# Attention and a small feed-forward block on eight cores: the last two token tiles one by one, bias rows by an accumulating DMA, query weights loaded sooner, and 53 instead of 43 tiles of exponentials on VectorE

## The reference

```python
def attn(x):                                   # x: (4, 4096, 1024)
    q = einsum('bnd,hkd->bnhk', x, query_proj) # 16 heads of 64
    k = einsum('bmd,dk->bmk', x, key_proj)     # one key head, shared
    v = einsum('bmd,dv->bmv', x, value_proj)   # one value head, shared
    p = softmax(einsum('bnhk,bmk->bnhm', q, k) / 8)
    return einsum('bnhv,dhv->bnd', einsum('bnhm,bmv->bnhv', p, v), output_proj)
def ffn(x):
    s = einsum('btd,dm->btm', x, Win) + bin_   # 64 wide
    h = relu(s[..., None] * W1 + b1)           # 16 hidden values for each
    return einsum('btm,md->btd', einsum('btmh,mh->btm', h, W2) + b2, Wout) + bout
x = x + attn(layernorm(x))
x = x + ffn(layernorm(x))
```

## Time and profile before

| | before |
|---|---|
| median of runs, us | 969.49 |
| profiled execution, us | 971.45 |
| its span, first to last instruction, slowest core | 969.9 |
| spans of the eight cores | 965.8 to 969.9 |
| ScalarE busy | 94% |
| TensorE busy | 93% |
| VectorE busy | 67% |
| GpSimd busy | 7% |
| DMA, mean | 50 GB/s |

### The profile page before, as it was taken

How to read it: one execution, slowest core, us unless ns; L and a number is a source line. 1 busy time by engine, 2 the same in 40 slices (tenths; PEclk the granted TensorE clock), 3 DMA queues, 4 the chain that set the end, 5 groups by cost and what they waited for, 6 DMA issues and landing times.

```text
span 969.9 us, 29153 instructions; the slowest of 8 cores (965.8 to 969.9 us)
## 1 busy us (share of the span) xinstructions
PE 900.7 (93%) x11484; PEld 479.2 (49%) x11484; DVE 646.1 (67%) x938; ACT 913.9 (94%) x1000; POOL 72.2 (7%) x150
## 2 busy tenths in 40 slices
PE   3899999999999999998999999998999998998895
PEld 3445555554445554554555554554454454454442
DVE  4756777522469999988889899658332378748225
ACT  2599999999999999999999999999999999999971
POOL 3211112100000000000010000000000000100000
PEclk9999999999999999999999999999999999999995
DMA  8722346400100010001031000001130100500101
GB/s 194 183 73 89 110 142 135 97 2 2 28 18 19 18 19 17 3 7 51 29 115 18 18 18 14 7 7 50 36 108 18 29 13 7 180 18 18 50 2 44
DMA packets 46291, 48.71 MB, mean 50 GB/s; under 512 B 35152, under 2 KB 35280, under 8 KB 46160
## 3 DMA queue, kind: packets, MB, share of 16 engines
q1 hardware_dynamic: 38352, 27.71, 10.4%
q0 software_dynamic: 7520, 18.62, 7.6%
q10 hardware_dynamic: 288, 0.52, 0.1%
HBM read 35.70 MB, written 8.39 MB: 45 GB/s over the span
## 4 chain that ended last, share of the span: by engine, by line
ACT 78%; issue 11%; PE 7%; DVE 2%; DMA 2%; POOL 0%; DVEq 0%; SPq 0%; ACTq 0%; POOLq 0%
ACT ptu L1163 77%; PE ob L731 2%; DMA xbuf<-x_own 1%; PE spa L1030 1%; DMA wqb<-wq 1%; PE spb L1030 1%; PE spb L1067 0%; PE spa L1067 0%; PE sdb L664 0%; DVE lnst L753 0%; DVE lnst L757 0%; PE sdb L695 0%; PE sda L695 0%; ACT hz L1173 0%; DVE gacc L1132 0%
## 5 line engine op out<-in xcount | busy, mean ns | idle before, releaser
L1163 ACT ACTIVATE ptu<-spa 128x1024 bf16<-128x1024 f32 x491 | 555.3, 1131 | 11.5 <-PE spa L1030 11.3
L1163 ACT ACTIVATE ptu<-spb 128x1024 bf16<-128x1024 f32 x490 | 555.8, 1134 | 3.6 <-PE spb L1030 3.3
L731 PE MATMUL ob<-vab,ptu 128*128 128x65 bf16 x7848 | 391.7, 195 | 3.4 <-DVE oacc L943 1.1
L731 PEld LDWEIGHTS ob<-vab,ptu 128*128 128x128 bf16 x7848 | 286.7, 98 | 203.8 <-issue 203.8
L1030 PE MATMUL spb<-qt,k2t 64*128 64x512 bf16 x980 | 193.5, 382 | 19.4 <-ACT ptu L1163 18.0
L1030 PE MATMUL spa<-qt,k2t 64*128 64x512 bf16 x982 | 193.6, 383 | 17.9 <-ACT ptu L1163 14.9
L1030 PEld LDWEIGHTS spb<-qt,k2t 64*128 64x128 bf16 x980 | 58.7, 92 | 110.7 <-issue 95.9
L1030 PEld LDWEIGHTS spa<-qt,k2t 64*128 64x128 bf16 x982 | 57.7, 93 | 108.5 <-issue 95.0
L943 DVE TENSOR_TENSOR oacc<-oacc,ob 128x520 f32<-128x520 f32 x52 | 35.8, 689 | 76.4 <-PE ob L731 76.3
L1184 POOL TENSOR_SCALAR lnve<-lnmv 128x1 f32<-128x1 f32 x48 | 14.9, 311 | 582.1 <-DVE lnmv L759 582.0
L929 DVE SCALAR_TENSOR_TENSOR r1t<-oacc 128x1024 bf16<-128x1024 f32 x43 | 52.6, 1223 | 5.2 <-DVE oacc L924 4.7
(11 more groups left out here) (136 smaller groups left out, 705.3 us busy)
## 6 DMA issues: line engine op xcount, KB each, us to landing
xbuf<-x_own SPq DMA_DIRECT2D x16, 512.0 KB, 5.2
xbuf<-x_oth SPq DMA_DIRECT2D x16, 512.0 KB, 3.4
out<-xbuf POOLq DMA_DIRECT2D x14, 512.0 KB, 3.1
xbuf<-x_own POOLq DMA_DIRECT2D x12, 512.0 KB, 7.1
wqb<-wq POOLq DMA_DIRECT2D x8, 256.0 KB, 9.3
xtra<-x_own SPq DMA_DIRECT2D x4, 512.0 KB, 6.6
xtra<-wp POOLq DMA_DIRECT2D x8, 256.0 KB, 4.7
ot<-on SPq DMA_TRANSPOSE x38, 2.3
```

Source lines behind the costliest of these rows:

```text
L731: r = te.matmul(osum[:, hd, c * 65:(c + 1) * 65], ptu[:, g % NPT, hd * 512 + c * 128:hd * 512 + (c + 1) * 128], vab[:, CHUNKS[s][i], :], s ...
L1163: sc.activation(ptu[:, g % NPT, :], sps[g % 2][:], AF.Exp, scale=0.125 / SCORE_SCALE).then_inc(ex, 1)
```

## The change

Five parts.

1. The table `OFF` holds 19, 20 and 14 tiles for passes 1 to 3: 53 on VectorE and 971 on ScalarE. `AT_FIRST` starts the play's clocks 140 of its units sooner. As the whole order comes from the play, the order of all later work is made anew.
2. The add of the bias row (line 840, 28 instructions on VectorE) goes. In its place GpSimd issues, for each token tile, a DMA that adds all of `boutbc` (512 KB, in SBUF) onto `xbuf`; it waits for the tile's norm, and the add of the layer's output waits for it. The store waits for that last add.
3. Query weights: the loads of `wvb` and head pair 1 are issued after the norm factor of tile 1, not 2; that of head pair 2 after tile 2, not 3. On VectorE the norm of tile 1 stands ahead of the statistics of tile 2.
4. The end: no bias matmuls; both tiles' adds and statistics come ahead of both norms; the hidden layer is done for tile 14 and then for tile 15, with twice as many operations of 128 columns.
5. The bias matmuls' row of ones goes.

```diff
-OFF = {1: [1, 2, 3, 2, 3, 2, 2, 2], 2: [2, 2, 3, 2, 2, 2, 2, 2], 3: [2, 0, 0, 2, 1, 2, 1, 1]}
+OFF = {1: [2, 3, 2, 3, 2, 1, 2, 4], 2: [2, 4, 2, 3, 2, 3, 2, 2], 3: [1, 0, 2, 2, 1, 3, 3, 2]}
-AT_FIRST = {"pe": 2100, "dve": 2200}
+AT_FIRST = {"pe": 1960, "dve": 2060}
...
                     xh = xbuf[:, t, b * 512:(b + 1) * 512]
+                    if b == 0:
+                        v.wait_ge(bad[t], 16 * (a // 4 + 1))
                     v.tensor_tensor(xh, xh, bank[:], op=ALU.add).then_inc(sev, 1)
-                    note("sev", n + 1)
-                    yield [], 75
-                    v.wait_ge(sev, n + 1)
-                    if a == 0 and b == 0:
-                        v.wait_ge(boutl, 16)
-                    v.tensor_tensor(xh, xh, boutbc[:, b * 512:(b + 1) * 512], op=ALU.add).then_inc(bad, 1)
...
-            for n, t in enumerate(GROUPS[-1]):
-                te.wait_ge(xad, n + 1)
-                for h in range(2):
-                    te.matmul(sps[t % 2][:, h * 512:(h + 1) * 512], ones1[:],
-                              boutbc[0:1, h * 512:(h + 1) * 512], start=True, stop=False)
+            def transposes(n, t):
                 te.wait_ge(nrm, NTILES + t + 1)
...
+            def hidden(n, t):
+                te.wait_ge([rta, rtv][n], 1)
+                for j in range(DCH):
+                    r = te.matmul(obk[:, 512 * n:512 * n + 128], winb[:, j, :],
+                                  r2t[:, j, t % 4 * 128:t % 4 * 128 + 128],
+                                  start=(j == 0), stop=(j == DCH - 1))
+                r.then_inc(s2t, 1)
...
+            ta, tb = GROUPS[-1]
+            transposes(0, ta)
+            hidden(0, ta)
+            transposes(1, tb)
+            hidden(1, tb)
+            ffn_out(0, ta)
+            ffn_out(1, tb)
...
             ln_stats(v, 1)
             ln_norm(v, 0)
+            ln_norm(v, 1)
             ln_stats(v, 2)
-            ln_norm(v, 1)
             ln_stats(v, 3)
...
                 ln_stats(v, li)
-                ln_norm(v, li)
+            for t in GROUPS[-1]:
+                ln_norm(v, NTILES + t)
...
+            for p in range(4):
+                hidden_sum(0, p)
             v.wait_ge(rtt, 2)
             v.tensor_copy(r2t[:, :, 384:512], side[1][:, :].bitcast(BF16).rearrange("p (j t) -> p j t", t=128)
                           ).then_inc(rtv, 1)
+            for p in range(4, 8):
+                hidden_sum(0, p)
             for p in range(8):
...
+                hidden_sum(1, p)
+            for n, t in enumerate(GROUPS[-1]):
+                v.wait_ge(bad[t % 4], 16 * NK)
...
+            for n in range(2):
+                sc.wait_ge(s2t, n + 1)
+                for p in range(8):
+                    if p >= 4:
+                        sc.wait_ge(gtl, 7 * n + p - 3)
+                    sc.activation(zt[p % 4][:, 128 * n:128 * n + 128], obk[:, 512 * n:512 * n + 128], AF.Relu,
+                                  bias=b1adj[:, p:p + 1], scale=w1p[:, p:p + 1]).then_inc(rel, 1)
...
+        def add_bout(e, t):
+
+            if t == 0:
+                e.wait_ge(boutl, 16)
+            e.wait_ge(nrm, NTILES + t + 1)
+            e.dma_start(xbuf[:, t % 4, :], boutbc[:], accum_op=ALU.add).then_inc(bad[t % 4], 16)
...
-                if i == 2:
+                if i == 1:
                     e.dma_start(wvb[:], wv_d.rearrange("p (j m) -> p j m", m=64)).then_inc(wvl, 16)
-                for c in {2: [1], 3: [2, 3], 4: [4], 5: [5], 6: [6], 7: [7]}.get(i, []):
+                for c in {1: [1], 2: [2], 3: [3], 4: [4], 5: [5], 6: [6], 7: [7]}.get(i, []):
...
                 for t in ts:
-                    e.wait_ge(bad, 2 * t + 2)
+                    add_bout(e, t)
+                for t in ts:
+                    wait_ev(e, USE_NO["fo", t, 1])
                     e.dma_start(out_r[t], xbuf[:, t % 4, :]).then_inc(ost[t % 4], 16)
...
             for t in GROUPS[-1]:
                 rstd_of(e, NTILES + t)
+            for t in GROUPS[-1]:
+                add_bout(e, t)
             for q in range(4):
+                e.wait_ge(bad[q], 16 * NK)
                 e.wait_ge(ost[q], 16 * (NK if q < 2 else NK - 1))
```

More of the change, by code:

```diff
@@ L533, in build_nc @@
         rsd = sem("rstd_set")
-        bad = sem("bout_added")
+        bad = [sem(f"bout_added{q}") for q in range(4)]
         b1s = sem("b1adj_set")
@@ L1074, in _, with ffn_out @@
                 r.then_inc(rtt, 1)
-            te.wait_ge(rta, 1)
-            te.wait_ge(rtv, 1)
-            for j in range(DCH):
-                r = te.matmul(obk[:, 0:256], winb[:, j, :], r2t[:, j, 256:512],
-                              start=(j == 0), stop=(j == DCH - 1))
-            r.then_inc(s2t, 1)
-            te.wait_ge(g2c, len(GROUPS))
-            for t in GROUPS[-1]:
+            def hidden(n, t):
[5 more added lines that the diff above has]
+                r.then_inc(s2t, 1)
+            def ffn_out(n, t):
+                te.wait_ge(g2c, len(GROUPS) + n)
                 for h in range(2):
@@ L1119, in _, with hidden_sum @@
                 ln_stats(v, li)
-                ln_norm(v, li)
+            for t in GROUPS[-1]:
+                ln_norm(v, NTILES + t)
+            def hidden_sum(n, p):
+                cols = slice(128 * n, 128 * n + 128)
+                last = slice(256 + 128 * n, 384 + 128 * n)
+                v.wait_ge(rel, 8 * n + p + 1)
+                dst = g2b[:, last] if p == 7 else gacc[p % 2][:, cols]
+                if p == 0:
+                    v.tensor_scalar(dst, zt[p % 4][:, cols], w2p[:, p:p + 1], b2h[:], op0=ALU.mult,
+                                    op1=ALU.add).then_inc(gtl, 1)
+                else:
+                    v.wait_ge(gtl, 7 * n + p)
+                    v.scalar_tensor_tensor(dst, zt[p % 4][:, cols], w2p[:, p:p + 1],
+                                           gacc[(p + 1) % 2][:, cols],
+                                           op0=ALU.mult, op1=ALU.add).then_inc(g2c if p == 7 else gtl, 1)
+            for p in range(4):
+                hidden_sum(0, p)
             v.wait_ge(rtt, 2)
@@ L1168, in _ @@
                           AF.Copy).then_inc(rta, 1)
-            sc.wait_ge(s2t, 1)
-            for p in range(8):
-                if p >= 4:
-                    sc.wait_ge(gtl, p - 3)
-                sc.activation(zt[p % 4], obk[:, 0:256], AF.Relu, bias=b1adj[:, p:p + 1],
-                              scale=w1p[:, p:p + 1]).then_inc(rel, 1)
+            for n in range(2):
[5 more added lines that the diff above has]
+                                  bias=b1adj[:, p:p + 1], scale=w1p[:, p:p + 1]).then_inc(rel, 1)
             for n, t in enumerate(GROUPS[-1]):
```

16 lines of the change are left out of this document (2 added, 14 removed).

## The result

The changed kernel takes 973.22 us (median of 7 runs, 971.87 lowest), the kernel before 970.26 beside it: the ratio is 1.0035 with a 95% interval of 1.0022 to 1.0047. That is within the 2% that count as no change, but it is a small loss, 3.0 us between the medians, where 12.7 us of gain were forecast, and it lies outside the range of 953 to 965. The slowest core of the profiled execution is core 6.

What follows compares the result with a forecast made beforehand. The prediction took ScalarE to bound the kernel: a start, 0.92 us for each tile, and an end. Ten tiles 9.2, start 2.0 and end 1.5 sum to 12.7 off the median 969.49: 956.8 us, range 953 to 965.

Steps and rivals of the forecast that it cites:

- The ten tiles, 9.2 us: Passes 1 to 3: ten more tiles leave ScalarE at 0.92 us each, VectorE and TensorE having room; 9.2 us gained.
- The bias by DMA: Passes and end: accumulating DMAs replace VectorE's adds, hidden before their use; beside the tile's transpose a loss of 0, at most 2.
- the tightest case is tile 13: Passes: its transpose, landed in 3.1 us, has 3 us to spare before use; 4.7 was the slowest.
- The start, 2.0 us: Before the 25th exponential: two waits, 3.3 us, mostly go through sooner weights; 2.0 us gained, bounds 0 and 3.3.
- Its first half: Start: head pair 1's weights are issued about 4 us sooner, so TensorE's 2.06 us wait goes, or nearly.
- The sign of being wrong that named the 17th exponential: Start: the forecast is wrong if the 17th exponential still starts near 49.
- Lower bound 0: Start: at worst another chain gives back all of the gain, leaving 0.
- The end, 1.5 us: After the last exponential: tile 15's adds start near 964.6 instead of 965.90; 1.5 us gained, upper bound 2.5.
- The bias late at the end: End: the accumulating DMA needs twice a load's time, tile 15's adds start about 3 us late: 959.8; chance 0.18.
- "Order, not load": Start or passes: TensorE waits in fixed order for VectorE or a transpose; 959 to 964, centre 961; chance 0.20.
- the middle term: Passes: the ten tiles' gain between start and end, 9.2 us, with 5 as its lower bound.
- The slower rival: End: the accumulating DMA lands so late that the kernel loses, from about 25 us; 972 at 27; chance 0.03.

Runs made afterwards that it cites:

- e4: The kernel before with the 53-tile table and the passes' bias by DMA, issued behind the transposes; start and end as before: 963.53 us, 0.994.
- e1: The changed kernel with a group's bias DMAs in passes 1 to 3 issued only when that group's transposes have landed: 964.49 us, 0.9946.
- e6: The changed kernel with each tile's bias DMA issued right behind its norm, not in a burst per group: 965.86 us, 0.9939.
- e7: e1 with only the planner's clocks (`AT_FIRST`) put back; sooner weights and norm 1 ahead of statistics 2 kept: 961.63 us, 0.990.
- e8: e1 with the whole start as before (weights, norm, clocks): 963.16 us, 0.991.
- e2: The kernel before with only the bias added by accumulating DMA in the passes; old table, start and end: 984.84 us, 1.0155.
- e5: The changed kernel with the bias DMAs of tiles 8 to 15 as plain 512 KB copies into free memory, leaving out their bias: 971.79 us, 0.9992.
- e10: e7 with each of the residual buffers' reloads waiting until the one before it has landed: 958.62 us, 0.9883.

## Why the prediction was wrong

- **The ten tiles, 9.2 us: right.** The last exponential of e4 is 9.3 us sooner, though its medians show 6.0. VectorE's work fitted into its idle time, and TensorE's places sufficed: with the bias DMAs out of the way (e1, e4, e6, e7, e8) the three passes lose 2.7 to 4.2 us, of which 1.5 to 2.9 are the pass of the wait near 500, against 2.8 in before.
- **The bias by DMA, "a loss here is 0, at most 2": this step failed.** It cost 8.4 us in pass 3 beside the ten tiles, and 13.1 alone (e2, 15.3 us by the medians). The step asked when the bias is wanted, and that was answered rightly: no add waited for it. What the DMA does to the transpose it put at no more than the slowest transpose in the trace, 4.7 us. But in that trace none of the row's 14 transposes has any of GpSimd's DMAs in flight beside it, so the row bounded nothing. Also, "the tightest case is tile 13": the last tile of a whole group is the one that meets the burst. GpSimd issues its four DMAs once the last norm factor is made. The last norm is made from that same factor, and both the last transpose and the fourth bias DMA wait for it. So they start together by construction: on every core of after two bias DMAs stand 1.6 and 0.7 us ahead of tile 11's transpose, and two 0.04 and 0.65 us behind it. Tile 13 met two DMAs; it landed after 7.4 us on core 6 and was used 7.9 us after its issue. On cores 2, 4 and 7 it landed after 8.7 to 9.1 us, and TensorE waited 0.8 to 1.2 there: within the step's "at most 2".
- **The start, 2.0 us: failed.** Its first half held: the second exponential follows the first by 0.92 us, the load is issued at 13.32 instead of 15.80, and e7 against e8 gives 1.1 us. The sign of being wrong that named the 17th exponential came true: it still starts near 49, at 48.58 after a wait of 3.42 us, and as a mean over the cores 24.9 us behind the first, against 24.7 in before. What the sum left out is that the clocks alter the planner's order behind the second exponential, for 2.6 us more. Lower bound 0 was the mistake: an order that is planned anew can lose.
- **The end, 1.5 us: right.** The tail is 1.27 us shorter, and e8 against e4, which have the same start and the same passes, gives 1.6. Executions differ in it too: before and e4 end alike in the code and stand 0.7 apart. The four kernels with the old end have tails of 30.6 to 31.7 us and the eight with the new one 29.8 to 30.3, 1.1 between the means.
- **The bias late at the end (rival, 0.18): it isn't.** The core 6 rows of the end answer:

```profile
954.51 1.21 POOL L1210 DMA_DIRECT2D xbuf<-boutbc_s  x1
...
956.49 0.86 POOL L1210 DMA_DIRECT2D xbuf<-boutbc_s  x1 [0.77 <-issue]
...
957.29 2.90 ACT L1190 ACTIVATE hz<-ob,b1adj,w1p_s 128x128 f32<-128x128 f32 x8 [1.26 <-PE ob L1070]
...
965.78 1.28 DVE L1154 TENSOR_TENSOR xbuf<-xbuf,spa 128x512 f32<-128x512 f32 x2
...
966.97 1.28 DVE L1154 TENSOR_TENSOR xbuf<-xbuf,spb 128x512 f32<-128x512 f32 x2
```

  The bias of tile 14 has 11.3 us, that of tile 15 10.5, and neither add waits. They land after 5.3 and 5.9 us, less than the load's time that the sum took (7.1), and far from twice it. Beside e5's copies at the same place, 3.3 and 3.5 us (near the 3 that the prediction put for a copy), the accumulating form takes 1.65 times as long. "Collectives: The Full Stack" of the Trainium skill, section "Part 3: Why 7x under link rate", has an add in the DMA path at half the rate of a copy; the runs come near that, and the forecast applied it to the wrong base, a load from HBM.
- **"Order, not load" (rival, 0.20) was the nearest.** It named where the time would go, TensorE in its fixed order in front of a transpose, but gave it half of the middle term: 961, not 973. Its cause was another: order costs 2.6 us at the start, and in pass 3 it was the transfer beside the transpose, since e1 has after's order of work on TensorE and no wait.
- **The slower rival named the right DMA in the wrong place.** It looked for an accumulating DMA that is late for its own reader, from 25 us on; the one that cost time was early, and made another transfer late.

With its causes removed most of the forecast's 12.7 us comes back: e10 is 0.9883 of before, 11.3 us (9.8 to 12.8) less than 970.2. 1.4 us of them are the wait near 500, which before doesn't have. e10 keeps the sooner weights, the ten tiles and the tail; it drops the clocks, and adds two kinds of waits on GpSimd, for the transposes and from reload to reload, of which no exponential's start shows a cost.
